# A five-sweep graph network in fp32: eleven rows of sweep 1 closed by feature, and all block sums on VectorE

## The chip, the core and the metric

The kernel runs on one core of a Trainium2 chip. Its time is the device time of one execution in microseconds; the figure of a kernel is the median of its runs. Engines are called by their short names where rows of the trace are shown: PE is TensorE (PEld its weight loads), DVE is VectorE, ACT is ScalarE, POOL is GpSimd, SP issues the loads of the adjacency matrix.

## The reference

`x` is 8192 nodes by 64 features, `adj` is 8192 by 8192, all fp32. Four residual layers follow each other, each on `h = relu(layernorm(x))`:

```python
# layer 0, two hops
for k in range(2):
    agg = adj @ x
    x = tanh(concatenate([agg, x], axis=1) @ W[k])
# layer 1
adj @ (x @ weight) + bias
# layer 2
adj @ (x * (u >= 0.1) / 0.9)
# layer 3
concatenate([x, (adj @ x) / (adj.sum(axis=1) + 1)], axis=-1) @ W.T
```

So `adj` is multiplied five times by a matrix of 64 columns, each one depending on the one before.

## The kernel before, in words

**Tiling.** `adj` is cut into 16 x 16 blocks of 512 x 512, 1 MB each, which lie transposed in memory. The block (i, j) adds the nodes j to the output row i. There are five *sweeps*, one for each product with `adj`; sweep 1 and 3 go down the rows (i = 0 to 15), sweeps 2, 4 and 5 up. A block that is loaded is used for two sweeps where both operands are known by then: with the row of the next sweep (`double`, two products, 8 matmuls of 512 columns), or alone (`single` or `late`, 8 matmuls of 256 columns, "narrow" below; `early` blocks of sweep 1 are two products as well). `operand` holds the values of the nodes, 64 columns for the odd sweeps and 64 for the even ones.

**Sevens.** In sweeps 2 and 3 most double blocks are made as *sevens* (`seven_products`, L961): a product of 2 x 2 half blocks with 7 multiplications in place of 8. For this, each block needs sums of its quarters, t1 and t3 (one subtraction of 1024 columns, L1372), t2 (512 columns, L1373) and t4 (512 columns, L881), each made from the one before. Before the change t4 is GpSimd's: it waits for `second_sum_made`, which t2 raises on VectorE, and raises `sums_made`, on which TensorE waits before the product. The three sum buffers are used in turn, so a sum is made at most three sevens ahead. VectorE also combines the operands of a block column once (`combine`, L1355 to L1358), and mixes a row's results at its end (`mix`, `mixed`, `take_doubles`, L1386 to L1429). In a row the first block, and in short rows the fourth too, is a plain double block, as is the last.

**Closing a row.** `post` multiplies a row's sums (`stack`, by feature: features on partitions, 512 nodes along the columns) with the weights and leaves them by node in PSUM (`natural`, L1025: 8 matmuls of 64 columns). In sweeps 1 and 2 ScalarE takes the tanh of it; in sweep 1 it goes straight to `operand`. In the other sweeps `finish` on VectorE adds it to the residual and normalizes. The own value of a node (the `x` in the concatenation) must stand by feature in the other half of `stack`: `turn_in_squares` (L1291) transposes it with 8 VectorE instructions from `operand`.

**What sets the order.** A list written out at build time (`make_plan`, then `with_sevens`) holds steps such as `block`, `post`, `turn`, `first`, `doubles`, `sums7`, `combine`; each engine walks through it and does its part, in order, with semaphores between engines. SP loads the blocks in the order in which they are used, into 13 slots (8 as long as the block sums of sweep 1 and the sevens hold the other five).

VectorE further adds up the columns of `adj` for the degrees: of the blocks on and below the diagonal in sweep 1 (`add_below`, L1233, L1239, L1240), which needs the early and double blocks there.

## Time and profile before

| | |
|---|---|
| median of 3 runs | 2221.46 us (2221.43 to 2221.57) |
| the profiled execution | 2219.71 us, its span 2217.9 us |
| TensorE busy | 2181.0 us, 98% of the span, granted clock 1.00 |
| VectorE busy | 1767.2 us, 80% |
| GpSimd busy | 289.7 us, 13% |
| ScalarE busy | 173.5 us, 8% |
| read from HBM | 834.90 MB, 377 GB/s over the span |

Sweep 1 lasts until about 680 us, sweep 2 until about 1100, sweep 3 until about 1535, sweep 4 until about 2140, and the rest is sweep 5. The shares are means over all of this; a wait is read from the rows of its own stretch. In a row of the trace, the bracket at the end is how long the engine sat idle before the row and what released it.

### The profile page before, as it was taken

How to read it: one execution, taken by the hardware profiler on the slowest of the kernel's cores; microseconds unless marked ns; L12 is line 12 of the kernel's file. 1: busy time of each engine (PE TensorE's matmuls, PEld its weight loads, DVE VectorE, ACT ScalarE, POOL GpSimd, SP SyncE). 2: the span in 40 equal slices, each digit the busy share in tenths (PEclk: the TensorE clock that was granted, in tenths of full speed). 3: DMA queues.
4: the chain of work that ended last, by engine and by line, in shares of the span. 5: the costliest groups of instructions: out<-in, count | busy, mean ns of one | idle time of the engine just before them, and what ended most of it. 6: DMA issues, size and time to landing. Idle time of an engine off the chain costs nothing.

```text
span 2217.9 us, 38303 instructions
## 1 busy us (share of the span) xinstructions
PE 2181.0 (98%) x15854; PEld 1235.5 (56%) x15854; DVE 1767.2 (80%) x3200; ACT 173.5 (8%) x388; POOL 289.7 (13%) x184
## 2 busy tenths in 40 slices
PE   6999999999999999999999999999999999999999
PEld 3555555555555467777755667676344444444446
DVE  7467777777887689999767889897888877778777
ACT  1000000000002321111100000000100000000000
POOL 0000000000000124343302344453000000000000
PEclk9999999999999999999999999999999999999999
DMA  9999999999999889999999999999899999999997
GB/s 397 421 420 418 419 415 413 399 399 405 400 379 363 301 322 333 346 350 350 345 420 350 342 335 353 338 327 364 356 397 410 409 411 407 397 410 398 415 400 308
DMA packets 118765, 839.50 MB, mean 379 GB/s; under 512 B 14016, under 2 KB 16320, under 8 KB 17088
## 3 DMA queue, kind: packets, MB, share of 16 engines
q1 hardware_dynamic: 114480, 832.62, 95.3%
q8 instruction: 126, 2.06, 0.4%
q10 hardware_dynamic: 3344, 2.33, 0.3%
q0 software_dynamic: 768, 2.10, 0.3%
q14 instruction: 47, 0.39, 0.0%
HBM read 834.90 MB, written 2.10 MB: 377 GB/s over the span
## 4 chain that ended last, share of the span: by engine, by line
PE 91%; DVE 4%; DMA 2%; issue 1%; POOL 1%; ACT 0%; SPq 0%; DVEq 0%; POOLq 0%
PE double_acc L933 33%; PE single_acc L961 20%; PE single_acc L905 16%; PE spare L933 14%; PE spare L905 7%; DMA store<-in_adj 2%; PE natural L1025 1%; DVE store L1372 1%; POOL store L881 1%; DVE store L1373 0%; DVE stats L1169 0%; PE spare L1038 0%; DVE partial L1272 0%; DVE partial L1403 0%; DVE partial L1429 0%
## 5 line engine op out<-in xcount | busy, mean ns | idle before, releaser
L933 PE MATMUL double_acc<-store,operand 128*64 128x512 f32 x3632 | 808.9, 592 | 1.2 <-ACT operand L1137 1.2
L933 PEld LDWEIGHTS double_acc<-store,operand 128*64 128x64 f32 x3632 | 280.3, 137 | 435.2 <-issue 414.3
L961 PE MATMUL single_acc<-store 128*64 128x256 f32 x2528 | 485.2, 379 | 0.0
L961 PE MATMUL single_acc<-store,operand 128*64 128x256 f32 x1944 | 452.1, 379 | 9.8 <-POOL store L881 9.8
L905 PE MATMUL single_acc<-store,operand 128*64 128x256 f32 x3696 | 438.7, 381 | 21.3 <-DVE operand L1205 11.9
L881 POOL TENSOR_TENSOR store<-store 128x512 f32<-128x512 f32 x162 | 279.7, 1726 | 1126.5 <-DVE store L1373 1126.4
L905 PEld LDWEIGHTS single_acc<-store,operand 128*64 128x64 f32 x3696 | 293.1, 138 | 189.0 <-issue 85.0
L961 PEld LDWEIGHTS single_acc<-store 128*64 128x64 f32 x2528 | 311.5, 137 | 40.9
L933 PE MATMUL spare<-store,operand 128*64 128x512 f32 x1456 | 330.3, 592 | 0.7 <-DMA store<-in_adj 0.7
L961 PEld LDWEIGHTS single_acc<-store,operand 128*64 128x64 f32 x1944 | 263.5, 137 | 70.7 <-issue 18.2
L1272 DVE TENSOR_TENSOR partial<-spare,partial 64x256 f32<-64x256 f32 (+1 forms) x250 | 126.4, 506 | 162.5 <-PE spare L933 109.7
L1372 DVE TENSOR_TENSOR store<-store 128x1024 f32<-128x1024 f32 x162 | 216.3, 1335 | 14.1 <-PE single_acc L961 8.1
L933 PEld LDWEIGHTS spare<-store,operand 128*64 128x64 f32 x1456 | 125.1, 137 | 149.8 <-issue 142.0
L1373 DVE TENSOR_TENSOR store<-store 128x512 f32<-128x512 f32 x162 | 188.1, 1161 | 5.6
L1233 DVE TENSOR_TENSOR deg_part<-store 128x1024 f32<-128x1024 f32 x133 | 162.0, 1218 | 11.7 <-DMA store<-in_adj 10.4
L905 PE MATMUL spare<-store,operand 128*64 128x256 f32 x1424 | 169.0, 379 | 0.0
L905 PEld LDWEIGHTS spare<-store,operand 128*64 128x64 f32 x1424 | 107.9, 137 | 71.0 <-issue 34.8
L1258 DVE TENSOR_TENSOR deg_part<-deg_part,store 128x1024 f32<-128x1024 f32 x105 | 128.6, 1225 | 3.6
L1257 DVE TENSOR_TENSOR deg_part<-deg_part,store 128x1024 f32<-128x1024 f32 x105 | 127.5, 1214 | 1.0
L1272 DVE TENSOR_TENSOR partial<-single_acc,partial 64x256 f32<-64x256 f32 x136 | 57.3, 422 | 56.1 <-PE single_acc L905 53.4
L1239 DVE TENSOR_TENSOR store<-store,deg_part 128x512 f32<-128x512 f32 x117 | 81.0, 692 | 4.0
L1240 DVE TENSOR_TENSOR store<-store,deg_part 128x512 f32<-128x512 f32 x117 | 81.0, 692 | 4.0
(88 smaller groups left out, 934.7 us busy)
## 6 DMA issues: line engine op xcount, KB each, us to landing
store<-in_adj SPq DMA_DIRECT2D x792, 1024.0 KB, 8.3
for_layer<-in_u POOLq DMA_DIRECT2D x16, 128.0 KB, 6.2
out_rows<-resid ACTq DMA_DIRECT2D x15, 128.0 KB, 5.9
resid<-in_x SPq DMA_DIRECT2D x2, 512.0 KB, 6.1
resid<-in_x SPq DMA_DIRECT2D x1, 1024.0 KB, 13.5
out_rows<-resid ACTq DMA_DIRECT2D x2, 64.0 KB, 1.7
w_stack<-in_w_both ACTq DMA_DIRECT2D x2, 32.0 KB, 8.7
ident<-in_identity ACTq DMA_DIRECT2D x1, 64.0 KB, 16.3
```

The costliest lines, as they stand in the source:

```text
L881: nc.gpsimd.tensor_tensor(t4, inside(at + 2 * BLOCK, (BLOCK, 2)), t2, ALU.subtract).then_inc(sums_made, 1)
L905: last = nc.tensor.matmul(acc[half_of(h), 0:HALF], operand[:, b.j * TPB + t, half_of(b.row.half)], stream[:, t, nodes_of(h)], start=b.firs ...
L933: last = nc.tensor.matmul(acc[half_of(half), :], operand[:, b.j * TPB + t, half_of(half)], stream[:, t, :], start=b.first and t == 0, stop ...
L961: last = nc.tensor.matmul(acc[half_of(half), nodes_of(nodes)], weights[:, t, :], data[:, t, :], start=first and k in (0, 2), stop=final an ...
L1233: nc.vector.tensor_tensor(deg_part[:, :], data[:, 0:2 * BLOCK], data[:, 2 * BLOCK:], ALU.add).then_inc(deg_added, 1)
L1239: link(nc.vector.tensor_tensor(to, to, deg_part[:, 0:BLOCK], ALU.add))
L1240: link(nc.vector.tensor_tensor(to, to, deg_part[:, BLOCK:], ALU.add))
L1257: link(nc.vector.tensor_tensor(acc, acc, data[:, 0:2 * BLOCK], ALU.add))
L1258: nc.vector.tensor_tensor(acc, acc, data[:, 2 * BLOCK:], ALU.add).then_inc(deg_added, 1)
L1272: return nc.vector.tensor_tensor(to, got, to, ALU.add)
L1372: link(nc.vector.tensor_tensor(t1_t3, y12_y22, y11_y12, ALU.subtract))
L1373: nc.vector.tensor_tensor(t2, y22, t1, ALU.subtract).then_inc(second_sum_made, 1)
```

## The change

It has four parts.

1. **Rows 0 to 10 of sweep 1 are closed by feature** (`BY_FEATURE`). The post of such a row is 2 matmuls of 256 columns with the weights as the stationary operand; ScalarE writes the tanh by feature to `partial`, and VectorE transposes it to `operand` (`to_nodes`, 8 instructions). The blocks of the next row that need this operand start after its fifth block and no longer after its third (fourth in row 1).
2. **The own value of sweep 2 is kept so**: in rows 0 to 10 of sweep 2 ScalarE copies it from `partial` to `stack`, and the 8 transposes there go.
3. **VectorE makes t4**, and GpSimd has only its loads of `u`.
4. **The order in sweeps 2 and 3**: three narrow blocks of sweep 4 (diagonal blocks 4, 5 and 6) stood after the rows 5, 6 and 7 of sweep 3; they now stand behind the second seven of rows 9, 13 and 14 (`BELOW_IN`). Row 6 of sweep 2 and row 15 of sweep 3 make their fourth block plain, so there are 160 sevens and not 162. Where the row after is not one of sevens, a `combine` stands right behind its `post` and no longer behind the `doubles`.

```diff
+BELOW_IN = {9: 4, 13: 5, 14: 6}
-ALL_SEVEN_OVER = 8
+ALL_SEVEN = {2: range(6), 3: range(9, NB - 1)}
+BY_FEATURE = range(11)
...
-        if row.own and not row.sevens:
+        if row.own and (not row.sevens or with_kept_own(row)):
             at[min(1, n_single)].append(("turn", row))
...
+        if row.sweep == 3 and row.i in BELOW_IN:
+            at[PLAIN_FIRST + SEVENS_BEFORE_PLAIN].append(lambda: late(4, BELOW_IN[row.i], [BELOW_IN[row.i]]))
...
-        begin = 3 if row.i == 1 else 2
+        begin = 4 if row.i - 1 in BY_FEATURE else 2
...
+            if row.r and n == min(at_first + 1, len(row.single) - 1) and by_feature(ROWS[row.r - 1]):
+                plan.append(("nodes", ROWS[row.r - 1]))
...
-            combines.append(("combine", of))
+            (combines if of.r + 1 in of_row else steps).append(("combine", of))
...
-                if what == "sums7":
-                    n, at = SEVEN_BLOCKS.index(of), LOAD_OF[of.number].slot * SLOT
-                    _, t2, t4 = block_sums(of)
-                    wait_loaded(pool.wait_ge, of)
-                    pool.wait_ge(second_sum_made, n + 1)
-                    nc.gpsimd.tensor_tensor(t4, inside(at + 2 * BLOCK, (BLOCK, 2)), t2, ALU.subtract).then_inc(sums_made, 1)
...
+                if by_feature(row):
+                    for h in range(2):
+                        last = nc.tensor.matmul(acc[half_of(h), 0:HALF], w_stack[:, row.sweep - 1, :], stacked[:, nodes_of(h)],
+                                                start=True, stop=True)
+                    last.then_inc(posted, 1)
+                    return
...
+                elif what == "turn" and with_kept_own(row):
+                    wait_stack(act.wait_ge, row)
+                    mine = half_of(1 - row.half)
+                    nc.scalar.copy(stack[mine, slot, :], partial[mine, row.i, :]).then_inc(own_copied, 1)
...
+                    if by_feature(row):
+                        act.wait_ge(posted, posts(row.r))
+                        for h in range(2):
+                            last = nc.scalar.activation(partial[half_of(row.half), row.i, nodes_of(h)],
+                                                        natural[slot][half_of(h), 0:HALF], ACT.Tanh)
+                        last.then_inc(tanh_ready, 1)
...
+            def to_nodes(row):
+                dve.wait_ge(tanh_ready, row.r + 1)
+                for c in range(F // SQUARE):
+                    at = row.half * F + c * SQUARE
+                    values = partial[at:at + SQUARE, row.i, :].rearrange("p (t n) -> p t n", t=TPB)
+                    for q in range(QUARTERS):
+                        part = slice(q * SQUARE, (q + 1) * SQUARE)
+                        last = nc.vector.transpose(operand[part, tiles(row.i), F + c * SQUARE:F + (c + 1) * SQUARE], values[:, :, part])
+                last.then_inc(nodes_ready, 1)
...
                 link(nc.vector.tensor_tensor(t1_t3, y12_y22, y11_y12, ALU.subtract))
-                nc.vector.tensor_tensor(t2, y22, t1, ALU.subtract).then_inc(second_sum_made, 1)
+                link(nc.vector.tensor_tensor(t2, y22, t1, ALU.subtract))
+                nc.vector.tensor_tensor(t4, y21, t2, ALU.subtract).then_inc(sums_made, 1)
```

Three places of the instruction order, of before and of the change. First TensorE in sweep 1 from the last two double blocks of row 3 into row 4 (`single_acc` are row 4's own narrow blocks, `spare` the early ones, `natural` the post of row 3), before:

```order
L933 MATMUL double_acc1<-store,operand 64x512 x16
L905 MATMUL single_acc0<-store,operand 64x256 x16
L1025 MATMUL natural1<-w_stack,stack 64x64 x8
L905 MATMUL single_acc0<-store,operand 64x256 x8
L933 MATMUL spare0<-store,operand 64x512 x8
L905 MATMUL single_acc0<-store,operand 64x256 x8
L933 MATMUL spare1<-store,operand 64x512 x8
```

and with the change:

```order
L961 MATMUL double_acc1<-store,operand 64x512 x16
L933 MATMUL single_acc0<-store,operand 64x256 x16
L1050 MATMUL natural1<-stack,w_stack 64x256 x2
L933 MATMUL single_acc0<-store,operand 64x256 x24
L961 MATMUL spare0<-store,operand 64x512 x8
L933 MATMUL single_acc0<-store,operand 64x256 x8
L961 MATMUL spare1<-store,operand 64x512 x8
```

Two more narrow blocks stand between the post and the first early block, which reads the operand that the post makes.

VectorE at the same place (the transposes to `stack` are row 4's own value, `deg_part` and `store` the degree sums), before:

```order
L1424 TENSOR_TENSOR stack<-double_acc1,stack 64x512
L1272 TENSOR_TENSOR partial<-double_acc1,partial 64x512
L1291 STREAM_TRANSPOSE stack<-operand 32x4x32 x8
L1233 TENSOR_TENSOR deg_part<-store 128x1024
L1239 TENSOR_TENSOR store<-store,deg_part 128x512
```

and with the change:

```order
L1476 TENSOR_TENSOR stack<-double_acc1,stack 64x512
L1318 TENSOR_TENSOR partial<-double_acc1,partial 64x512
L1337 STREAM_TRANSPOSE stack<-operand 32x4x32 x8
L1362 STREAM_TRANSPOSE operand<-partial 32x4x32 x8
L1279 TENSOR_TENSOR deg_part<-store 128x1024
L1285 TENSOR_TENSOR store<-store,deg_part 128x512
```

The new transposes stand directly behind the row's own ones, ahead of the next degree sum.

VectorE in row 13 of sweep 3, from the operand of row 12 on, which is followed by the sums of the fourth and later blocks of the row, before:

```order
L1508 SCALAR_TENSOR_TENSOR operand<-centred,keep 128x4x64
L1372 TENSOR_TENSOR store<-store 128x2x2x256
L1373 TENSOR_TENSOR store<-store 128x2x256
L1372 TENSOR_TENSOR store<-store 128x2x2x256
L1373 TENSOR_TENSOR store<-store 128x2x256
L1372 TENSOR_TENSOR store<-store 128x2x2x256
```

and with the change:

```order
L1560 SCALAR_TENSOR_TENSOR operand<-centred,keep 128x4x64
L1423 TENSOR_TENSOR store<-store 128x2x2x256
L1424 TENSOR_TENSOR store<-store 128x2x256
L1425 TENSOR_TENSOR store<-store 128x512
L1423 TENSOR_TENSOR store<-store 128x2x2x256
L1424 TENSOR_TENSOR store<-store 128x2x256
L1425 TENSOR_TENSOR store<-store 128x512
L1318 TENSOR_TENSOR partial<-spare1,partial 64x256 x2
L1423 TENSOR_TENSOR store<-store 128x2x2x256
```

Each sum has three instructions there, and the taking of the narrow block (`partial<-spare1`) stands behind the second sum.

## Rows read from the trace of the kernel before

**Rows 1.** Who waited for whom, whole program: us in total, times, longest us

```profile
PE single_acc L961 <- POOL store L881: 9.8, 7, 2.4
```

**Rows 2.** The same view of the stretch from 1180 to 1600 us

```profile
PE single_acc L961 <- POOL store L881: 7.0, 5, 1.6
```

**Rows 3.** Stretches, sweep 3, row 13: us busy by engine, clock, DMA

```profile
1375.00:1430.00 55.00, 53.38 (x476) 39.65 (x473) 50.87 (x59) 1.46 (x3) 30.97 (x16) 1.00 0.94 339
```

**Rows 4.** Costliest groups of the page: busy us, mean ns | idle before, releaser

```profile
L1373 DVE TENSOR_TENSOR store<-store 128x512 f32<-128x512 f32 x162 | 188.1, 1161 | 5.6
...
L1239 DVE TENSOR_TENSOR store<-store,deg_part 128x512 f32<-128x512 f32 x117 | 81.0, 692 | 4.0
```

**Rows 5.** Chain of waits, sweep 3, rows 10 and 11: start us, us, piece

```profile
1285.32 6.87 PE double_acc L933 x32
1292.18 0.47 PE natural L1025 x16
1292.65 6.05 PE single_acc L961 x56
1298.69 1.73 PE spare L905 x16
```

**Rows 6.** Timeline of VectorE, sweep 3, rows 12 and 13: start us, us

```profile
1394.61 0.68 DVE L1386 TENSOR_TENSOR stack<-single_acc,partial 64x512 f32<-64x512 f32 x1 [2.31 <-PE single_acc L961]
...
1400.16 1.22 DVE L1372 TENSOR_TENSOR store<-store 128x1024 f32<-128x1024 f32 x1
1401.42 0.69 DVE L1373 TENSOR_TENSOR store<-store 128x512 f32<-128x512 f32 x1
...
1404.84 0.41 DVE L1485 TENSOR_TENSOR resid<-resid,bias_sb 128x256 f32<-128x256 f32 x1
...
1408.15 1.22 DVE L1372 TENSOR_TENSOR store<-store 128x1024 f32<-128x1024 f32 x1
```

**Rows 7.** Timeline of GpSimd, the same row 13

```profile
1410.26 2.10 POOL L881 TENSOR_TENSOR store<-store 128x512 f32<-128x512 f32 x1 [1.17 <-DVE store L1373]
```

**Rows 8.** Timeline of TensorE, the same row 13, products j3 and j4

```profile
1407.65 0.38 PE L961 MATMUL single_acc<-store,operand 128*64 128x256 f32 x1
...
1412.50 0.40 PE L961 MATMUL single_acc<-store,operand 128*64 128x256 f32 x1 [1.62 <-POOL store L881]
```

**Rows 9.** Timeline of VectorE, sweep 2, end of row 10

```profile
754.65 0.69 DVE L1424 TENSOR_TENSOR stack<-double_acc,partial 64x512 f32<-64x512 f32 x1 [8.29 <-PE double_acc L933]
...
756.44 1.22 DVE L1372 TENSOR_TENSOR store<-store 128x1024 f32<-128x1024 f32 x1
```

**Rows 10.** Timeline of TensorE, first product of seven in sweep 2

```profile
760.78 0.40 PE L961 MATMUL single_acc<-store,operand 128*64 128x256 f32 x1 [2.38 <-POOL store L881]
```

**Rows 11.** Timeline of TensorE, sweep 1, row 4

```profile
273.79 0.66 PE L1025 MATMUL natural<-w_stack,stack 128*64 128x64 f32 x16
...
275.99 3.63 PE L933 MATMUL spare<-store,operand 128*64 128x512 f32 x16
```

**Rows 12.** Timeline of VectorE, the same row 4

```profile
274.31 2.53 DVE L1291 STREAM_TRANSPOSE stack<-operand 32x128 f32<-32x128 f32 x8
276.87 1.22 DVE L1233 TENSOR_TENSOR deg_part<-store 128x1024 f32<-128x1024 f32 x1
```

**Rows 13.** Timeline of TensorE's weight loads, the same row 4

```profile
275.77 0.39 PEld L933 LDWEIGHTS spare<-store,operand 128*64 128x64 f32 x4
```

**Rows 14.** Timeline of TensorE, sweep 1, row 1

```profile
63.00 3.65 PE L933 MATMUL spare<-store,operand 128*64 128x512 f32 x16 [0.66 <-DMA store<-in_adj]
66.46 1.93 PE L905 MATMUL single_acc<-store,operand 128*64 128x256 f32 x16
```

**Rows 15.** Timeline of VectorE, sweep 2, rows 14 and 13

```profile
707.72 0.86 DVE L1272 TENSOR_TENSOR partial<-spare,partial 64x256 f32<-64x256 f32 x2
```

**Rows 16.** Timeline of TensorE, sweep 2, row 13's closing

```profile
711.74 0.63 PE L1025 MATMUL natural<-w_stack,stack 128*64 128x64 f32 x16
```

**Rows 17.** Timeline of ScalarE, sweep 2, row 14

```profile
704.30 1.43 ACT L1137 ACTIVATE operand<-resid,shift,rsd 128x64 f32<-128x64 f32 x4 [0.44 <-DVE shift L1192]
```

More of the change, by code:

```diff
@@ L116, in __init__ @@
             first, end = PLAIN_FIRST, len(self.double) - PLAIN_END.get((self.sweep, i), 1)
-            between = first + SEVENS_BEFORE_PLAIN if len(self.double) <= ALL_SEVEN_OVER else None
+            between = first + SEVENS_BEFORE_PLAIN if self.i not in ALL_SEVEN[self.sweep] else None
             self.sevens = [j for n, j in enumerate(self.double) if first <= n < end and n != between]
@@ L122, with by_feature, with_kept_own, rows_by_feature @@
 ROW_OF = {(row.sweep, row.i): row for row in ROWS}
+def by_feature(row):
+    return row.sweep == 1 and row.i in BY_FEATURE
+def with_kept_own(row):
+    return row.sweep == 2 and row.i in BY_FEATURE
+def rows_by_feature(r):
+    return sum(by_feature(row) for row in ROWS[: r + 1])
+def rows_with_kept_own(r):
+    return sum(with_kept_own(row) for row in ROWS[: r + 1])
 class Block:
@@ L255, in downwards @@
     def downwards(row):
-        if row.sweep == 3 and row.i >= 1 and row.i - 1 not in FILL_UP[4] and row.i - 1 not in TURN:
+        if row.sweep == 3 and row.i >= 1 and row.i - 1 not in (*FILL_UP[4], *TURN, *BELOW_IN.values()):
             late(4, row.i - 1, [row.i - 1])
@@ L397, in with_sevens @@
                 combines.clear()
-                if of.row.own:
+                if of.row.own and not with_kept_own(of.row):
                     steps.append(("turn", of.row))
@@ L406, in with_sevens @@
         elif what == "doubles":
-            if of.r + 1 not in of_row or of.r not in of_row:
-                steps.extend(combines)
-                combines.clear()
             sums7(of_row.get(of.r + 1, [])[:SUMS])
@@ L572, in rows_in_squares @@
 def rows_in_squares(r):
-    return sum(row.own and not turned_by_tensor(row) for row in ROWS[: r + 1])
+    return sum(row.own and not turned_by_tensor(row) and not with_kept_own(row) for row in ROWS[: r + 1])
 def added_to(row):
@@ L827, in wait_partial, with wait_stack @@
                 wait_saved(wait_ge, before.r)
+        def wait_stack(wait_ge, row):
+            if closed_by_tensor(ROWS[row.r - 2]):
+                wait_ge(posted, posts(row.r - 2))
+            else:
+                wait_ge(turned_back, rows_turned_back(row.r - 2))
         def wait_operand(wait_ge, sweep, j):
@@ L832, in wait_operand @@
                 wait_ge(first_ready, j * TPB // GROUP + 1)
+            elif sweep == 2 and by_feature(ROW_OF[1, j]):
+                wait_ge(nodes_ready, rows_by_feature(ROW_OF[1, j].r))
             elif sweep == 2:
@@ L875, in _ @@
             for what, of in PLAN:
-                if what == "sums7":
-                    n, at = SEVEN_BLOCKS.index(of), LOAD_OF[of.number].slot * SLOT
-                    _, t2, t4 = block_sums(of)
-                    wait_loaded(pool.wait_ge, of)
-                    pool.wait_ge(second_sum_made, n + 1)
-                    nc.gpsimd.tensor_tensor(t4, inside(at + 2 * BLOCK, (BLOCK, 2)), t2, ALU.subtract).then_inc(sums_made, 1)
-                elif what == "post" and 2 * NB <= of.r + 2 < 3 * NB:
+                if what == "post" and 2 * NB <= of.r + 2 < 3 * NB:
                     row = ROWS[of.r + 2]
@@ L1007, in post @@
                     wait_new(own_ready, rows_with_own(row.r))
+                elif with_kept_own(row):
+                    wait_new(own_copied, rows_with_kept_own(row.r))
                 elif row.own:
@@ L1098, in _ @@
             for what, row in PLAN:
-                if what in ("block", "added", "added_both", "combine", "sums7", "mixed", "close_upper", "close_below", "degree"):
+                if what in ("block", "added", "added_both", "combine", "sums7", "mixed", "close_upper", "close_below", "degree", "nodes"):
                     continue
@@ L1125, in _ @@
                         load_constants()
-                    if row.sweep <= 2:
+                    if by_feature(row):
[4 more added lines that the diff above has]
+                        last.then_inc(tanh_ready, 1)
+                    elif row.sweep <= 2:
                         act.wait_ge(posted, posts(row.r))
@@ L1293, in turn_in_squares @@
                     last.then_inc(squares_ready, 1)
-            def wait_stack(row):
-                if closed_by_tensor(ROWS[row.r - 2]):
-                    dve.wait_ge(posted, posts(row.r - 2))
-                else:
-                    dve.wait_ge(turned_back, rows_turned_back(row.r - 2))
             def turn_back(row):
@@ L1319, in take_first @@
                 if 2 <= row.r < (SWEEPS - 1) * NB:
-                    wait_stack(row)
+                    wait_stack(dve.wait_ge, row)
                 part = half_of(row.half)
@@ L1379, in mix @@
                 mine = half_of(row.half)
-                wait_stack(row)
+                wait_stack(dve.wait_ge, row)
                 wait_partial(dve.wait_ge, row)
@@ L1414, in take_doubles @@
                 else:
-                    wait_stack(row)
+                    wait_stack(dve.wait_ge, row)
                     wait_partial(dve.wait_ge, row)
@@ L1539, in _ @@
                         add_along(part, DEGREE_BLOCKS.index(of), of)
-                elif what == "turn" and not turned_by_tensor(of):
+                elif what == "nodes":
+                    to_nodes(of)
+                elif what == "turn" and not turned_by_tensor(of) and not with_kept_own(of):
                     turn_in_squares(of, range(F // SQUARE - 1) if of is ROWS[-1] else range(F // SQUARE))
```

9 lines of the change are left out of this document (5 added, 4 removed).

## The prediction, on record before the run

> **What bounds the kernel now.** I read the list of waits first, by engine, then the table of stretches, then the chain, and last the timelines around the waits that the change touches. TensorE is busy in 98% of the span at a granted clock of 1.00, so only two things can move the time: TensorE's work and TensorE's gaps. A gap that the change can close is one that names its releaser. For the products of seven (L961) there are seven of these, 9.8 us in all, released by GpSimd's fourth sum [rows 1]; five of them, 7.0 us, lie in sweep 3 [rows 2], where TensorE has 1.6 us of gap in a stretch of 55 us while VectorE is busy for 50.9 us of it and GpSimd for 31.0 us [rows 3]. VectorE is thus close behind TensorE there, and the question is whether it can take GpSimd's part. The loads are no bound in these sweeps (339 GB/s, share 0.94). Only at the start of sweep 1 TensorE waits for them [rows 14].
>
> **The waits of the sevens, a gain.** In row 13 of sweep 3 the product j3 starts at 1407.65. A product of seven takes 3.02 us (56 instructions for two, 6.05 us [rows 5]), so j4 was due at 1410.67. It starts at 1412.50, when GpSimd's sum (1410.26, 2.10 us) is done [rows 7, 8]. The loss is 1.83 us, of which the view calls 1.62 us a wait; 0.21 us goes with the restart. For all seven waits this gives 9.8 + 7 x 0.21 = 11.3 us.
>
> What would be late next is VectorE's own chain. A sum is now three dependent subtractions: 1.26 us from the start of the first to the second [rows 6], then 0.69 us and a gap of 0.03, then 0.69. The value 0.69 is that of the same shape in sweep 1, where GpSimd does nothing (L1239, 692 ns), and not the 1161 ns that L1373 has as a mean [rows 4]. In row 13 the t2 at 1401.42 has no GpSimd sum beside it and takes 0.69 too [rows 6]. So a sum costs 2.66 us, against 3.02 us of TensorE. In row 13: two sums from 1400.16 on end at 1405.5, the closing of row 12 takes 1408.15 - 1404.84 = 3.31 us, to 1408.8, and the sum of j4 is ready at 1411.5, or 1411.6 with 0.14 us from the sum's end to TensorE's start (1412.36 to 1412.50 [rows 7, 8]). That alone would leave 0.9 us of the wait of 1.83. But the narrow block of sweep 4 now stands ahead of j4: 1.73 us [rows 5], so j4 is due at 1412.4, and the sum is 0.8 us early. Rows 9 and 14 have the same cover, row 15 has a plain block there. Rows 10 to 12 had a narrow block before and do not wait long enough to be among the seven.
>
> Over a whole row, VectorE needs 0.12 + 5.55 us for mixing and taking (from 1394.61 to 1400.16 [rows 6]), 2.66 us for each sum, 3.31 us for the closing, 1.1 us for the combination (from 754.65 to 756.44 less 0.69 [rows 9]) and 0.86 us for the narrow block [rows 15]. With 11 sums in row 13 this is 40.2 us; TensorE has 6.87 + 0.47 + 11 x 3.02 + 1.73 = 42.3 us [rows 5]. Row 9, with 7 sums, is the closest: 29.6 against 30.2 us. The narrow blocks that leave rows 6 to 8 are not missed: in row 6 of sweep 3, as in row 9 of sweep 2, the first sum comes right after the row before. In sweep 2 that is 754.65 + 0.72 + 2.66 + 0.14 = 758.2, because the combination no longer stands between, and TensorE is due at 760.78 - 2.38 = 758.4 [rows 9, 10]. The wait of 2.38 us goes.
>
> **Two sevens made plain, a cost.** A plain double block takes 3.43 us (6.87 for two) where a seven takes 3.02 [rows 5]: 2 x 0.41 = 0.8 us.
>
> **The start of sweep 1, a cost.** The first early block starts at 63.00, after 0.66 us of waiting for its load, and the next narrow one at 66.46 [rows 14]. Loads come one by one there, so one more narrow block ahead of the early one is paced by the load and not by its 1.73 us. That costs at least the 0.66 us, and 0.9 us if the load needs a full 2.6 us. I take 0.8 us. Later rows begin with two more narrow blocks each, which eat into the lead of the loads; no gap of TensorE behind 63.00 names a load, so I cost these at nothing. If the lead were short in row 2, another 0.8 us would go.
>
> **The transposes in sweep 1, a small cost.** In row 4 the row's own transposes start at 274.31 and end at 276.84; the new ones take as long, from 276.87 to 279.40 [rows 12]. ScalarE's two tanh pieces run from the end of the post (273.79 + 0.66 = 274.45 [rows 11]) and have 2.4 us, enough for them. The early block now starts two narrow blocks later, 275.99 + 2 x 1.73 = 279.45, less 0.04 for the shorter post. So operand and block arrive together. But TensorE's weights of this block, which are the operand, are loaded from 275.77 on, 0.22 us ahead of the block [rows 11, 13]. I therefore take 0.2 us for each of the eight rows (4 to 11) in which the transposes start 0.5 us behind the post, as here: 1.6 us. The bounds are nothing, if the load can be late, and 0.6 us a row (5 us). The Trainium skill says on its page "TensorE: Matmul & The Clock Gate" (section "Architectural detail: the array is 16× 32×32, not 1× 128×128") that TensorE pulls weight loads ahead of matmuls in flight. By that rule the wait of the first load is all in the open and the term is the 1.6 us; without it the term would be 0. The trace agrees with the rule: 0.22 us.
>
> VectorE has room in these rows, since it does the same number of transposes as before in all: 11 x 2.53 us come to sweep 1 and the same go from sweep 2. TensorE's post is 2 matmuls of 256 columns, side by side on two halves as in a narrow block (8 in 1.73 us), so 0.43 us against 0.47 [rows 5]: 11 x 0.04 = 0.4 us gained. If they ran one after the other it would be 0.87 us and 4.4 us lost; the form is that of the narrow blocks, so I leave this out.
>
> **The combination behind the post, a small cost.** In row 13 of sweep 2 VectorE now combines row 14's operand before it takes anything else. It must wait for ScalarE's ReLU, 704.30 + 1.43 = 705.73 [rows 17], and then needs 1.1 us. What ended at 707.72 + 0.86 = 708.6 [rows 15] ends 2.5 us later, at 711.1, the row's sum is taken at 711.8, and the post was due at 711.74 [rows 16]: 0.2 us, between 0 and 1.
>
> **Sum.** -11.3 + 0.8 + 0.8 + 1.6 - 0.4 + 0.2 = -8.3 us. The profiled execution took 2219.71 us, so the changed one should take 2211.4. The median of before is 1.75 us above its profiled execution; I add this: 2213.2 us.
>
> **Rivals.** *VectorE overflows in part.* The margins are 0.6 us in row 9, 0.8 us at j4 and 0.2 us at the first seven of sweep 2. If each sum costs 0.15 us more than I think (2.8), row 9 has 7 x 0.14 = 1.0 us more to do and is 0.4 us over, and small waits of some 0.5 us come back in eight or so of the 20 rows with sevens: 2213 + 4 = 2217 us. For it: VectorE's 50.9 of 55 us. Against it: 0.69 us is what each subtraction took where GpSimd was silent.
>
> *Given back in sweep 1.* If the operand comes a further microsecond late, because the end of a row on VectorE is pushed back too, eight rows cost 8 us more: 2221 us, no change. For it: operand and block arrive within 0.1 us. Against it: VectorE waits for early blocks in these rows, so it starts each row's end on time.
>
> *VectorE becomes the bound.* If the three subtractions cost what L1372 and L1373 show as means in sweeps 2 and 3, a sum takes about 1.3 + 1.16 + 1.16 = 3.65 us, 0.6 us more than TensorE's 3.02; over 160 sums this is 100 us: about 2310 us, far slower. It decides from about 2.9 us a sum. Against it: the long t2 stands only beside a running GpSimd sum (1161 ns against 692 [rows 4]). The Trainium skill (page "SBUF — State Buffer", section "SBUF: two separate sides") says that VectorE and GpSimd take a shared port pair in turn and that the loser waits for the whole instruction. By it this rival is void, as no GpSimd sum is left; the trace agrees as far as 1161 against 692 ns goes.
>
> **How the numbers follow.** My forecast gets 0.76, the partial overflow 0.12, the loss in sweep 1 0.08, the VectorE bound 0.04. The forecast's own range goes from 2210.5 (no cost in the transposes) to 2216.5 (0.6 us a row). The range of 8 in 10 reaches from 2210 to 2217.5 and takes in half of the partial overflow. A measurement of this kernel can tell about 0.2%, 4.4 us, from no change: below 2217.0 it is faster. That holds for the forecast and about half of the overflow, with a little of the forecast's upper end lost: 0.81. The rest of the overflow and most of the loss in sweep 1 give "same" 0.13, and slower is 0.06, the VectorE bound and a sweep 1 worse than priced.
>
> **What would show it.** No wait of TensorE for sums in sweeps 2 and 3, or only such under 0.3 us. VectorE's second and third subtraction at 0.69 us, and its busy time about where it was. In sweep 1, TensorE's early blocks starting 0.2 us after the last narrow one ends, with the transposes as releaser. The start of sweep 1 0.8 us later at the end of the first early pair. The forecast is wrong if j4 in rows 9, 13, 14 or 15 still waits, if the first sevens of rows 6 to 8 begin to wait, or if sweep 1 ends more than 4 us later than before.

## The result, and the profile after

| | before | changed |
|---|---|---|
| median | 2221.43 us (2219.64 to 2221.57, 6 runs) | 2209.17 us (2209.11 to 2209.19, 6 runs) |
| the profiled execution | 2219.71 us, span 2217.9 us | 2209.11 us, span 2207.3 us |

The changed kernel takes 0.9947 of the time before, interval 0.9934 to 0.996: 12.3 us faster, where 8.3 were forecast, and 0.8 us below the lower end of the range. From profile to profile it is 10.6 us. The 1.7 us between these two numbers has a cause of its own, told with the experiments. How much of it the medians show is partly luck: 4 of the 6 runs of before fell on its upper level, while two later sets of before, of 16 and 11 runs, have their medians at 2219.86 and 2219.81, on the lower one. Against those the changed kernel gains 10.6 to 10.7 us.

The page of the changed kernel, parts 1 and 5 (busy us, mean ns | idle before):

```profile
PE 2178.9 (99%) x15698; PEld 1210.0 (55%) x15698; DVE 1762.9 (80%) x3356; ACT 183.4 (8%) x410; POOL 9.8 (0%) x22
...
L1423 DVE TENSOR_TENSOR store<-store 128x1024 f32<-128x1024 f32 x160 | 195.2, 1220 | 10.5 <-PE single_acc L989 9.9
L1424 DVE TENSOR_TENSOR store<-store 128x512 f32<-128x512 f32 x160 | 110.7, 692 | 5.5
L1425 DVE TENSOR_TENSOR store<-store 128x512 f32<-128x512 f32 x160 | 110.7, 692 | 5.4
```

and of the page of before the row of t1 and t3:

```profile
L1372 DVE TENSOR_TENSOR store<-store 128x1024 f32<-128x1024 f32 x162 | 216.3, 1335 | 14.1 <-PE single_acc L961 8.1
```

VectorE has the 160 subtractions t4 more to make, 110.7 us, and still its busy time falls from 1767.2 to 1762.9 us. The mean of t2 went from 1161 ns to 692 [rows 4], which gives back 77.4 us, and that of t1 and t3 from 1335 to 1220, another 21.1 us; the rest came off other instructions that had run beside GpSimd, the combinations most of all (their second subtraction, L1356, fell from 17.8 to 6.4 us in all). L961 of before is L989 now. The list of waits of TensorE (us in total, times, longest) has no row for it any more:

```profile
PE single_acc L933 <- DVE operand L1251: 11.9, 1, 11.9
PE single_acc L933 <- DMA store<-in_adj: 10.5, 17, 1.4
PE double_acc L961 <- ACT operand L1183: 1.3, 3, 0.6
PE spare L961 <- DMA store<-in_adj: 0.6, 1, 0.6
PE natural L1061 <- DVE stack L1476: 0.4, 2, 0.2
```

All 9.8 us of [rows 1] are gone. (The 11.9 us is the wait for the very first operand, as before.) The stretch of [rows 3], with busy us of PE, PEld, DVE, ACT and POOL, then granted clock, share and GB/s of the DMA engines, shows TensorE without a gap and VectorE with 3 us less to do (the same work lies some 9 us sooner in the changed kernel, so the two stretches are alike and not equal):

```profile
1375.00:1430.00 55.00, 55.00 (x482) 38.53 (x480) 47.87 (x79) 2.62 (x5) 0.54 (x1) 1.00 0.96 352
```

VectorE's timeline there, from the sums of row 13 (the first pair answers to 1400.16 and 1401.42 of [rows 6]) past the closing of row 12 to the next sum:

```profile
1391.16 1.23 DVE L1423 TENSOR_TENSOR store<-store 128x1024 f32<-128x1024 f32 x1
1392.42 0.69 DVE L1424 TENSOR_TENSOR store<-store 128x512 f32<-128x512 f32 x1
1393.14 0.69 DVE L1425 TENSOR_TENSOR store<-store 128x512 f32<-128x512 f32 x1
1393.75 1.22 DVE L1423 TENSOR_TENSOR store<-store 128x1024 f32<-128x1024 f32 x1
...
1396.34 0.42 DVE L1537 TENSOR_TENSOR resid<-resid,bias_sb 128x256 f32<-128x256 f32 x1
...
1399.66 1.22 DVE L1423 TENSOR_TENSOR store<-store 128x1024 f32<-128x1024 f32 x1
```

From the start of one sum to the next it is 1393.75 - 1391.16 = 2.59 us, against 3.02 us of TensorE, and the closing 1399.66 - 1396.34 = 3.32 us. The forecast had 2.66 (to the end of the third subtraction, as here too) and 3.31.

TensorE and VectorE in row 4 of sweep 1, which answer to [rows 11, 12] (TensorE first, its weight load last):

```profile
274.37 0.63 PE L1050 MATMUL natural<-stack,w_stack 128*64 128x256 f32 x4
274.81 5.38 PE L933 MATMUL single_acc<-store,operand 128*64 128x256 f32 x48
279.99 3.63 PE L961 MATMUL spare<-store,operand 128*64 128x512 f32 x16
```

```profile
274.65 2.53 DVE L1337 STREAM_TRANSPOSE stack<-operand 32x128 f32<-32x128 f32 x8
277.21 2.51 DVE L1362 STREAM_TRANSPOSE operand<-partial 32x128 f32<-32x128 f32 x8
```

```profile
279.77 0.39 PEld L961 LDWEIGHTS spare<-store,operand 128*64 128x64 f32 x4
```

The transposes end at 279.72, the weights are loaded from 279.77, the early block starts at 279.99 without a wait. The load follows the operand by 0.05 us. All eight rows from 4 to 11 look like this: VectorE's own transposes start 0.27 to 0.28 us behind the post, where it was 0.51 to 0.52 before.

Where the time went, from the end of each sweep's last block in the two profiled executions:

| | before | changed | forecast |
|---|---|---|---|
| sweep 1 ends | 682.07 | 682.37: +0.3 | +2.0 |
| sweep 2 lasts | 418.24 | 415.34: -2.9 | |
| sweep 3 lasts | 434.36 | 426.25: -8.1 | -10.3 with sweep 2 |
| sweeps 4 and 5 last | 678.38 | 678.48: +0.1 | 0 |

### The profile page after: what moved, and what is told of

Same layout as the page of the kernel before. It is cut to its first block, busy times and chain, and to the rows that moved or that the text cites. A ratio compares the mean times of both kernels' runs of the same rounds, so it can differ in the third digit from the quotient of the medians.

```text
span 2207.3 us, 37828 instructions
## 1 busy us (share of the span) xinstructions
PE 2178.9 (99%) x15698; PEld 1210.0 (55%) x15698; DVE 1762.9 (80%) x3356; ACT 183.4 (8%) x410; POOL 9.8 (0%) x22
## 4 chain that ended last, share of the span: by engine, by line
PE 95%; DMA 3%; DVE 1%; ACT 0%; issue 0%; SPq 0%; DVEq 0%
PE double_acc L961 35%; PE single_acc L989 22%; PE single_acc L933 16%; PE spare L961 14%; PE spare L933 7%; DMA store<-in_adj 3%; PE natural L1061 1%; ACT operand L1183 0%; PE natural L1050 0%; PE spare L1074 0%; DVE stack L1337 0%; DVE partial L1318 0%; SPq L902 0%; DVE deg_part L1279 0%; DVE stack L1476 0%
## 5 line engine op out<-in xcount | busy, mean ns | idle before, releaser
L961 PE MATMUL double_acc<-store,operand 128*64 128x512 f32 x3664 | 815.3, 592 | 1.3 <-ACT operand L1183 1.3
L961 PEld LDWEIGHTS double_acc<-store,operand 128*64 128x64 f32 x3664 | 279.1, 137 | 443.8 <-issue 422.2
L989 PE MATMUL single_acc<-store 128*64 128x256 f32 x2496 | 478.5, 379 | 0.0
L933 PE MATMUL single_acc<-store,operand 128*64 128x256 f32 x3696 | 434.1, 380 | 22.5 <-DVE operand L1251 11.9
L989 PE MATMUL single_acc<-store,operand 128*64 128x256 f32 x1920 | 440.6, 379 | 0.0
L989 PEld LDWEIGHTS single_acc<-store 128*64 128x64 f32 x2496 | 306.2, 137 | 64.8 <-issue 2.1
L961 PE MATMUL spare<-store,operand 128*64 128x512 f32 x1456 | 326.2, 592 | 0.6 <-DMA store<-in_adj 0.6
L989 PEld LDWEIGHTS single_acc<-store,operand 128*64 128x64 f32 x1920 | 261.5, 137 | 50.0 <-issue 2.1
L961 PEld LDWEIGHTS spare<-store,operand 128*64 128x64 f32 x1456 | 125.7, 137 | 158.2 <-issue 152.3
L1423 DVE TENSOR_TENSOR store<-store 128x1024 f32<-128x1024 f32 x160 | 195.2, 1220 | 10.5 <-PE single_acc L989 9.9
L1279 DVE TENSOR_TENSOR deg_part<-store 128x1024 f32<-128x1024 f32 x133 | 162.1, 1218 | 10.5 <-DMA store<-in_adj 9.1
L1424 DVE TENSOR_TENSOR store<-store 128x512 f32<-128x512 f32 x160 | 110.7, 692 | 5.5
L1425 DVE TENSOR_TENSOR store<-store 128x512 f32<-128x512 f32 x160 | 110.7, 692 | 5.4
```

The costliest lines, as they stand in the source:

```text
L933: last = nc.tensor.matmul(acc[half_of(h), 0:HALF], operand[:, b.j * TPB + t, half_of(b.row.half)], stream[:, t, nodes_of(h)], start=b.firs ...
L961: last = nc.tensor.matmul(acc[half_of(half), :], operand[:, b.j * TPB + t, half_of(half)], stream[:, t, :], start=b.first and t == 0, stop ...
L989: last = nc.tensor.matmul(acc[half_of(half), nodes_of(nodes)], weights[:, t, :], data[:, t, :], start=first and k in (0, 2), stop=final an ...
L1279: nc.vector.tensor_tensor(deg_part[:, :], data[:, 0:2 * BLOCK], data[:, 2 * BLOCK:], ALU.add).then_inc(deg_added, 1)
L1423: link(nc.vector.tensor_tensor(t1_t3, y12_y22, y11_y12, ALU.subtract))
L1424: link(nc.vector.tensor_tensor(t2, y22, t1, ALU.subtract))
```

## The experiments

The runs ask three things: which part brings the gain; why sweep 1 cost nothing for the transposes; and why the median fell by 1.7 us more than the profile. No kernel leaves anything of the computation out.

**The kernel before, once more**, for the spread of its own time.

> The kernel before, unchanged, timed against itself. Its runs so far lie at two levels, 2219.6 to 2219.8 and 2221.4 to 2221.6 us, while all six runs of the changed kernel lie within 0.1 us. Theory: the upper level is one more wait of some 1.8 us for a GpSimd sum, in one row of sweep 3; a profile that falls on the upper level shows 10.6 to 12 us of such waits, one on the lower level the 9.8 us seen. Rival: the levels come from the start (the loads of row 0), and then the waits for sums are equal at both levels.

Measured: 2221.27 us (2219.66 to 2221.64, 11 runs), ratio 0.9999 [0.999, 1.0008]. The times have two levels and nothing between: 5 of its 11 runs lie at 2219.7 to 2219.9, 6 at 2221.3 to 2221.6, and of the 21 runs of before beside it 7 and 14. Of all 65 runs of this kernel 35 lie on the upper one. The profile ahead of the prediction was taken at the lower level, this one at the upper, span 2219.7 us. The stretch of 10 us around the first product of seven in sweep 2, in the profile of before:

```profile
755.00:765.00 10.00, 7.62 (x70) 4.80 (x68) 9.74 (x16) 3.08 (x4) 5.08 (x3) 1.00 0.61 221
```

and in this execution, with TensorE's timeline:

```profile
755.00:765.00 10.00, 7.62 (x54) 4.37 (x52) 9.75 (x16) 3.10 (x4) 5.07 (x3) 0.83 0.61 219
```

```profile
760.80 0.59 PE L961 MATMUL single_acc<-store,operand 128*64 128x256 f32 x1 [2.38 <-POOL store L881]
...
763.74 0.63 PE L961 MATMUL single_acc<-store,operand 128*64 128x256 f32 x1
...
764.45 0.38 PE L961 MATMUL single_acc<-store 128*64 128x256 f32 x1
```

The wait is the same 2.38 us. But behind it the matmuls take 0.63 us and not 0.38, up to 764.2: the granted clock is 0.5, its 1.2 GHz level, for 3.4 us. That costs 3.4 / 2 = 1.7 us, the distance of the levels. It follows TensorE's longest wait of the sevens.

So both guesses made beforehand were wrong: TensorE waits 9.8 us for GpSimd's sums at either level, in seven waits, and up to the wait at 758 us the two executions agree within 0.03 us. At 1093 us the upper one is 1.7 us behind.

**t4 on VectorE alone** (before, with nothing else of the change).

```diff
-                    nc.gpsimd.tensor_tensor(t4, inside(at + 2 * BLOCK, (BLOCK, 2)), t2, ALU.subtract).then_inc(sums_made, 1)
...
-                nc.vector.tensor_tensor(t2, y22, t1, ALU.subtract).then_inc(second_sum_made, 1)
+                link(nc.vector.tensor_tensor(t2, y22, t1, ALU.subtract))
+                nc.vector.tensor_tensor(t4, y21, t2, ALU.subtract).then_inc(sums_made, 1)
```

> Before, with t4 on VectorE and nothing else changed. Theory: in sweep 3 the four waits at j4 fall from 1.83 to about 0.9 us and the one at the first seven of row 6 goes (4.8 us gained); in sweep 2 the first seven waits 0.9 in place of 2.6 us, but rows 6 and 5 overflow VectorE (row 6: 7 sums of 2.66 us and 11.4 us of the rest make 30.0 us against TensorE's 28.5), 1.8 us lost. About 2214.5 to 2216 us. Rival (the waits went through the new order alone): no gain, 2220 to 2221.5. Rival (VectorE becomes the bound): above 2222.

Measured: 2212.54 us (2212.46 to 2212.64), ratio 0.9963 [0.995, 0.9975], span 2210.8 us. TensorE's waits for the sums, the whole program:

```profile
PE single_acc L954 <- DVE store L1367: 3.3, 5, 0.9
```

and two of them in its timeline, row 13 of sweep 3 and the first seven of sweep 2:

```profile
1407.37 0.40 PE L954 MATMUL single_acc<-store,operand 128*64 128x256 f32 x1 [0.60 <-DVE store L1367]
```

```profile
759.27 0.40 PE L954 MATMUL single_acc<-store,operand 128*64 128x256 f32 x1 [0.85 <-DVE store L1367]
```

With its restart j4 loses 0.82 us in rows 9, 13, 14 and 15 each; the prediction's "that alone would leave 0.9 us" was right. The overflow of 1.8 us expected in rows 6 and 5 of sweep 2 did not come, and the time is 2.0 us below the lower end expected here.

**The new order alone** (t4 stays with GpSimd).

```diff
+BELOW_IN = {9: 4, 13: 5, 14: 6}
-ALL_SEVEN_OVER = 8
+ALL_SEVEN = {2: range(6), 3: range(9, NB - 1)}
...
-            combines.append(("combine", of))
+            (combines if of.r + 1 in of_row else steps).append(("combine", of))
```

> Before, with the new order alone (narrow blocks in rows 9, 13, 14, two plain blocks, the combination behind the post), t4 still on GpSimd. Theory: the narrow block of 1.73 us covers all but 0.1 us of each j4 wait, the plain block the one of row 15, the first seven of sweep 2 waits 1.1 us less; row 6 of sweep 3 loses its cover and waits some 1.3 us; two plain blocks cost 0.8 us. About 2212.5 to 2214.5 us. Rival (only VectorE's sums help): the waits stay, 2220.

Measured: 2212.89 us (2212.88 to 2212.97), ratio 0.9964 [0.9952, 0.9977], span 2211.1 us.

```profile
PE single_acc L961 <- POOL store L881: 2.5, 2, 1.3
```

The narrow block ahead of j4 (in row 15 the plain block) cures those four waits by itself, but for 0.1 to 0.2 us in rows 9, 13 and 14; in the list only the first sevens of each sweep still wait. So the order alone takes 6.8 us off the span and t4 alone 7.1, together 10.5 (below): they are two cures of largely the same waits and do not add up.

**The parts by feature alone** (before, with parts 1 and 2 of the change).

```diff
+BY_FEATURE = range(11)
...
-        begin = 3 if row.i == 1 else 2
+        begin = 4 if row.i - 1 in BY_FEATURE else 2
```

> Before, with rows 0 to 10 closed by feature and the own value kept, GpSimd's t4 and the old order. Theory: sweep 1 is 0.3 us longer (0.65 at its start, 0.04 less for each of 11 posts), sweep 2 keeps its wait of 2.6 us at the first seven and loses the small ones (0.6 us); within 0.5 us of before. Rival: the freed 2.5 us of VectorE a row in sweep 2 are the gain, 3 us or more faster.

Measured: 2221.43 us (2219.66 to 2221.52, 11 runs), ratio 1.0 [0.9991, 1.0009], at the same two levels, with a span of 2217.9 us at the lower one, that of before. They bring nothing by themselves and cost nothing.

**The change without the parts by feature.**

```diff
-BY_FEATURE = range(11)
...
-        begin = 4 if row.i - 1 in BY_FEATURE else 2
+        begin = 3 if row.i == 1 else 2
```

> The changed kernel without its by-feature parts (sweep 1 and the own value as before), with VectorE's t4 and the new order. Theory: sweep 1 is 0.3 us shorter, and in sweep 2 the 2.5 us of transposes a row leave the first seven of row 8 waiting 0.6 us: 2209.2 to 2209.7, so the by-feature parts are worth nothing here. Rival (they are what makes room for t4 on VectorE): 2211 or more.

Measured: 2209.27 us (2209.25 to 2209.32), ratio 0.995 [0.9936, 0.9964], span 2207.4 us. All but 0.1 us of the gain is in parts 3 and 4. The post of row 9 of sweep 2 waits 0.34 us there, 0.56 with its restart, and sweep 1 is 0.3 us shorter; most of it cancels.

**The operand in sweep 1, later on purpose.** Two kernels put one memset on VectorE ahead of the new transposes, 0.27 us long in the first, 0.485 us in the second. If every delay of the weights' load is paid in full, the cost begins at 0.05 us of delay; if the load could be late up to the start of the block, at 0.27.

```diff
             def to_nodes(row):
 
+                for _ in range(1):
+                    nc.vector.memset(by_node[:, :, :], 0.0)
```

and in the second kernel

```diff
             def to_nodes(row):
 
+                nc.vector.memset(mixing, 0.0)
```

> The changed kernel with a VectorE memset of 128x256 ahead of the new transposes of each of the 11 rows, so that the operand comes that much later (its duration is read from the trace; some 0.2 to 0.35 us). Theory: the slack is 0.05 us, so each of rows 4 to 11 waits the memset's time less 0.05: 1.2 to 2.4 us slower. Rival (weights are needed later than they are loaded): no change under 0.2 us of delay a row.

Measured: 2210.86 us (2210.81 to 2211.01), ratio 0.9959 [0.9946, 0.9971], 1.7 us over the changed kernel. The weights of row 4's first early block, with the post of that row at 274.63:

```profile
280.38 0.20 PEld L961 LDWEIGHTS spare<-store,operand 128*64 128x64 f32 x4 [0.42 <-DVE operand L1364]
```

> The same with a memset of 128x512, about twice the delay (0.35 to 0.6 us). Theory: eight rows wait the memset's time less 0.05 us, 2.4 to 4.4 us slower; with the other run this gives a slope of 8 rows. Rival: VectorE's later row ends are late too, then the cost is more than 8 times the delay.

Measured: 2213.31 us (2213.23 to 2213.44), ratio 0.9969 [0.9958, 0.9981], 4.1 us over. Row 4 of sweep 1, TensorE, its weight load and VectorE:

```profile
274.94 0.60 PE L1050 MATMUL natural<-stack,w_stack 128*64 128x256 f32 x4
...
280.95 3.65 PE L961 MATMUL spare<-store,operand 128*64 128x512 f32 x16 [0.23 <-DVE operand L1363]
```

```profile
280.95 0.20 PEld L961 LDWEIGHTS spare<-store,operand 128*64 128x64 f32 x4 [0.69 <-DVE operand L1363]
```

```profile
277.89 0.48 DVE L1355 MEMSET scaled<- 128x512 f32 x1 [0.17 <-issue]
278.38 2.51 DVE L1363 STREAM_TRANSPOSE operand<-partial 32x128 f32<-32x128 f32 x8
280.93 1.23 DVE L1279 TENSOR_TENSOR deg_part<-store 128x1024 f32<-128x1024 f32 x1
```

The load follows the transposes' end (280.89) at once, and the block starts with it, no longer 0.22 us behind it. With the gaps around the memset the load comes 5.75 us behind the post in the first kernel and 6.01 in the second, where it was 279.77 - 274.37 = 5.40: it is 0.35 and 0.61 us late. From one post to the next, nine rows (2 and 4 to 11) lose 0.18 to 0.20 us each in the first and 0.44 to 0.48 in the second. So it is indeed the load that waits, at either delay, but some 0.16 us of its lateness cost nothing, and neither of the two rules above holds: by these rows the cost begins at about 0.16 us of delay. In both kernels the load starts 0.05 to 0.06 us behind the transposes' end, as it does in the changed kernel; so the 0.05 us there are the way from the one to the other, and no margin.

**The early blocks one narrow block sooner.**

```diff
-        begin = 4 if row.i - 1 in BY_FEATURE else 2
+        begin = 3 if row.i - 1 in BY_FEATURE else 2
```

> The changed kernel with the early blocks of sweep 1 one narrow block sooner (after the fourth block of a row, not the fifth). Theory (the operand is ready 0.05 us before TensorE loads it in rows 4 to 11): each of these eight rows now waits 1.7 us for it, rows 2 and 3 less, and only row 1 gains 0.65 us: about 15 to 17 us slower, 2224 to 2226. Rival (there is slack that the trace doesn't show): no more than 5 us slower.

Measured: 2224.23 us (2224.03 to 2224.61, 11 runs), ratio 1.0017 [1.0008, 1.0026], 15.1 us over the changed kernel. TensorE's list of waits, and its row 4:

```profile
PE spare L961 <- DVE operand L1362: 13.5, 10, 1.5
```

```profile
281.55 3.65 PE L961 MATMUL spare<-store,operand 128*64 128x512 f32 x16 [1.46 <-DVE operand L1362]
```

Rows 4 to 11 lose some 1.67 us each. The load comes 1.84 us later than it is due there, 1.73 for the narrow block and 0.11 because the transposes start 0.38 us behind the post and not 0.28; again 0.17 us of it cost nothing. The place of the early blocks is exact to one block.

**Only row 1 one narrow block sooner.**

```diff
+        begin = 3 if row.i == 1 else 4 if row.i - 1 in BY_FEATURE else 2
```

> The changed kernel with row 1 alone beginning its early blocks after its fourth block, as before the change. In row 1 the transposes end at 61.1 us and the early block would start at 62.8, so no wait for them. Theory (the start of sweep 1 is paced by loads, and the narrow block there costs 0.65 us): 0.65 us faster, 2208.5. Rival (the loads' lead is short in row 2 then, or the loss moves on): no change.

Measured: 2208.46 us (2208.37 to 2208.5), ratio 0.9948 [0.9935, 0.996], 0.7 us under the changed kernel. In row 1 the move is a loss, by the load that paces it.

**A wait put back where the longest one was.** In the changed kernel nine memsets, each waiting for the one before, stand ahead of the first sum of row 9 of sweep 2.

```diff
+                    if (of.row.sweep, of.row.i, of.j) == (2, 9, of.row.sevens[0]):
+                        for _ in range(9):
+                            link(nc.vector.memset(by_node[:, :, :], 0.0))
```

> The changed kernel with nine dependent VectorE memsets (0.27 us each, 2.7 us with the gaps) ahead of the first block sum of row 9 of sweep 2, so that TensorE waits about 2.4 us there, as in the kernel before at 758 to 761 us. Theory (such a wait is what lets the clock fall to half for 3.4 us afterwards): the wait costs 2.6 us in every run, 2211.8, and most runs a further 1.75 us, 2213.5; a two-level spread as before. Rival (the fall of the clock has to do with GpSimd or with the time since the start): one level, 2211.8.

Measured: 2214.12 us (2212.55 to 2215.56, 6 runs), ratio 0.9971 [0.996, 0.9983]. The wait came out at 3.3 us, where 2.4 were meant, so both levels lie 0.7 us or more above those expected. The times fall on levels again: 2 runs at 2212.6, 3 at 2214.1 to 2214.3, 1 at 2215.6 (its mean clock is 0.998, for 0.999 and 1.000 of the others, which would fit a second fall; no trace shows it). The profiled execution is of the middle level:

```profile
755.00:765.00 10.00, 6.68 (x48) 3.31 (x46) 8.46 (x17) 4.05 (x5) 0.00 (x0) 0.86 0.68 250
```

```profile
762.37 0.66 PE L989 MATMUL single_acc<-store,operand 128*64 128x256 f32 x1 [3.32 <-DVE store L1425]
```

The granted clock is 0.50 from 762.2 to 765.6, again 3.4 us.

**The same wait in sweep 3**, ahead of the first sum of row 6 (the 2 and 9 of the diff read 3 and 6).

> The same memsets ahead of the first sum of row 6 of sweep 3, some 1185 us into the run, so again a wait of about 2.4 us. Theory (length of the wait alone): two levels, 2211.8 and 2213.5. Rival (what stands before and behind the wait matters too, or the place in the run): one level at 2211.8.

Measured: 2214.33 us (2212.82 to 2214.54, 6 runs), ratio 0.997 [0.9959, 0.9982]: 2 runs at 2212.8 to 2212.9, 4 at 2214.2 to 2214.5. The profiled one is of the lower level, with a wait of 3.2 us and no fall of the clock, so that here the fall is read from the times (and a mean clock of 0.999 in the four upper ones) alone:

```profile
1188.55 0.40 PE L989 MATMUL single_acc<-store,operand 128*64 128x256 f32 x1 [3.19 <-DVE store L1425]
```

So the levels come back with a long wait, at either place, with VectorE as the releaser and nothing on GpSimd. The kernels above whose longest wait of the sevens is 0.9 or 1.3 us lie within 0.2 us of their median and have no levels, and the one with ten waits of up to 1.5 us in sweep 1 has none either in 11 runs. (Its 11 times span 0.6 us. They, and those of the other kernels here, are compared with 2209.17 us, which was not timed beside them; the lower level of before is 2219.6 to 2219.9 in every set.)

**What the runs point to.** Row 1 as above, and row 6 of sweep 2 keeps its seventh seven.

```diff
-ALL_SEVEN = {2: range(6), 3: range(9, NB - 1)}
+ALL_SEVEN = {2: range(7), 3: range(9, NB - 1)}
...
+        begin = 3 if row.i == 1 else 4 if row.i - 1 in BY_FEATURE else 2
```

> The changed kernel with row 1 of sweep 1 beginning its early blocks after the fourth block (0.7 us, as measured) and the seven of row 6 of sweep 2 kept (0.41 us; its sum is ready 0.7 us early by the measured 2.66 us a sum). Expected 2208.1 us. Rival (VectorE overflows in row 6): 2208.5 or more.

Measured: 2207.90 us (2207.8 to 2207.99), ratio 0.9944 [0.9931, 0.9956], span 2206.0 us. It beats both kernels: 1.3 us under the changed one, 0.7 from row 1 and 0.6 against the kernel with row 1 alone. Of the latter the seven is 0.40: row 6 of sweep 2 takes 28.49 us from post to post and 28.89 there. Another 0.15 us lies before the post of row 0 of sweep 1, where nothing was changed, and is no gain of the edit.

## Why the prediction was right, and where it failed

**The waits of the sevens: right.** Block by block the seven took 2.6, 0.6, 0.7 and 4 x 1.85 = 7.4 us, 11.3 in all, as forecast from 9.8 and seven restarts. VectorE did take over GpSimd's part with room: 2.59 us a sum, and the narrow block covers j4. What the step left out are waits of 0.1 to 0.2 us that are in no row of the view: the j4 of rows 10 to 12 of sweep 3 (0.39 together), and the second sevens of rows 5, 3, 2 and 1 in sweep 2 (0.41). They went too, 0.8 us.

**Two sevens made plain: right**, 0.4 us each; the best kernel shows 0.40 us for one of them in its row.

**The posts: right**, 0.43 us each for 0.47, so 0.4 us.

**The combination behind the post: right in size**, 0.27 us for 0.2.

**The start of sweep 1: right but a little dear.** 0.65 us for 0.8, as the next narrow block shows: it started at 66.46 before [rows 14], and 68.84 - 66.46 - 1.73 for the narrow block ahead of it is 0.65.

```profile
65.38 3.65 PE L961 MATMUL spare<-store,operand 128*64 128x512 f32 x16 [0.62 <-DMA store<-in_adj]
68.84 1.93 PE L933 MATMUL single_acc<-store,operand 128*64 128x256 f32 x16
```

**The transposes in sweep 1: wrong, the first step that failed.** The term was 1.6 us and it is nothing. Part of the mechanism held: the load of the operand runs ahead of its block, by 0.22 us, and the two delays show that it is the load that waits. The Trainium skill ("TensorE: Matmul & The Clock Gate", section "Architectural detail: the array is 16× 32×32, not 1× 128×128") has weight loads pulled ahead of matmuls, and the trace agrees. What was wrong is the start that I gave to the chain. I took it from before, 0.5 us behind the post (274.31 and 273.79). With the change it is 0.28 us behind (274.65 and 274.37). VectorE's end of a row is not tied to TensorE's post: it comes after VectorE's last wait for a block, by whatever work VectorE has from there on. Before, the last wait in row 3 was for this one:

```profile
258.61 0.69 DVE L1272 TENSOR_TENSOR partial<-spare,partial 128x512 f32<-128x512 f32 x1 [1.89 <-PE spare L933]
```

and in the changed kernel it is two early blocks sooner, since the early blocks lie otherwise among the narrow ones:

```profile
252.32 0.69 DVE L1318 TENSOR_TENSOR partial<-spare,partial 128x512 f32<-128x512 f32 x1 [1.88 <-PE spare L961]
```

From there VectorE works through. An early block's degree sum and taking are 3.31 us of it (258.34 to 261.65 in the changed kernel's VectorE timeline) where TensorE needs about 3.44, so each step without a pause gains it 0.13 us. Two of them are the 0.24 us by which the row's end comes nearer to the post, and the 0.2 us a row is gone, in all eight rows alike.

The price was also too high for the start that I took, since a late load is not paid in full. By the forecast the operand is ready at 279.40, and the block is due at 279.41 and its load 0.22 us sooner, at 279.19. The load would have come at 279.45, 0.26 us late. Less the 0.16 us that the three kernels above show to cost nothing, this is 0.1 us a row and 0.8 us in all, by an estimate from these rows, and not 1.6. The rival "given back in sweep 1" argued with the same rows; the experiment with one block less shows how near it was.

**The 1.75 us from profile to median: wrong, the second step that failed.** I carried the distance between before's profiled execution and its median over to the changed kernel as if it were a property of the measurement. It is a property of the kernel before: somewhat over half of its executions are 1.7 us longer, and the one of them that was profiled shows why: the clock falls once to the 1.2 GHz level for 3.4 us, behind the wait of 2.38 us. That wait is what the change removes, and the second level goes with it. The four kernels with a wait for sums of 2.4 us or more (before, the parts by feature alone, the two with memsets) have the levels, the ones without have not. The median gained 12.3 us, of which 10.6 are in the profile and 1.7 are this. Without the 1.75 us the forecast would have been 2211.4, still 2.2 us too high.

**The sum of the terms.** With what was measured it is -11.3 + 0.8 + 0.65 + 0 - 0.4 + 0.3 - 0.8 = -10.8 us, against -10.6 from profile to profile. The miss of 4.0 us is 1.75 for the level, 1.6 for the transposes, 0.8 for the short waits and 0.15 for the start, less 0.1 for the combination and 0.2 that stays open. The range had a slip too: its "2210.5 (no cost in the transposes)" does not follow from the forecast, 2213.2 - 1.6 is 2211.6.

**The rivals.** No sum on VectorE cost more than forecast, so neither overflow came about. The parts by feature alone give 1.0 in ratio: no gain was lost there.

What stays open: why the clock falls behind the same wait in some executions and not in others, and whether a wait between 1.6 us (four waits of before in sweep 3, with no fall behind them in either profile) and 2.4 us would bring it. This was not tried.

## What to carry to other kernels

If a profiled execution lies below the median by a fixed amount, look at all the single times for levels before you carry the difference over: a level belongs to a place in the kernel, and the change may remove it. To place a step that must just be in time, date it from the last wait of the engine that makes it, not from the engine that uses it; a moved block moves that wait. Before you charge the lateness of a weight load in full, delay it on purpose: here 0.16 us of it were free. And when an engine that shares work with another is relieved of it, price the partner's instructions as they are beside an idle neighbour.

## What the runs showed of the hardware

- One idle stretch of TensorE of 2.4 us, in a kernel in which it is busy for 98%, is followed in 35 of 65 executions by a time 1.7 us longer, and where such an execution was profiled, by 3.4 us at the 1.2 GHz level (matmuls of 256 columns 0.63 us long, 0.38 otherwise). Behind 3.3 us the trace shows the same; behind 3.2 us, in another place, the times do (4 of 6 runs each).
- The load of a late stationary operand waits for it, but not all of that is lost: loads 0.35, 0.61 and 1.84 us late cost 0.19, 0.46 and 1.67 us a row.
- VectorE and GpSimd slowed each other in fp32 subtractions. GpSimd's sum and VectorE's, in row 13 of sweep 3 of before, GpSimd first:

```profile
1405.07 1.32 POOL L881 TENSOR_TENSOR store<-store 128x512 f32<-128x512 f32 x1 [0.69 <-DVE store L1373]
```

```profile
1410.02 1.22 DVE L1372 TENSOR_TENSOR store<-store 128x1024 f32<-128x1024 f32 x1
1411.27 1.63 DVE L1373 TENSOR_TENSOR store<-store 128x512 f32<-128x512 f32 x1
```

The sum of 1410.26 [rows 7] starts while t1 runs (to 1411.24) and ends at 1412.36, 1.1 us behind it, where 1.3 us is its length at 1405.07, beside no long subtraction of VectorE; t2 starts in the trace at 1411.27 and ends at 1412.90, 0.54 us behind GpSimd's sum. The Trainium skill ("SBUF — State Buffer", section "SBUF: two separate sides") has the one fully blocked while the other runs; these rows agree with it to 0.2 us. So where the two met, GpSimd's t4 of 1.3 us cost VectorE's t2 0.94 us, more than the 0.69 us of making t4 itself. They met in half of the blocks: 80 of the 162 t2 are 1.63 to 1.65 us long in the trace, the others 0.69. Over all blocks VectorE is busy 111 us longer in before than with the change when t4 is left out of the latter (1767.2 against 1762.9 - 110.7, with 3.8 us for the two blocks more), 0.69 us a block: GpSimd's help cost VectorE as much time as it took off it.
